# A transformer block with four expert feed-forward rounds: gates to all partitions through a DRAM row, rounds written out

## The chip, the cores and the metric

The kernel runs on one core of one Trainium2 chip. The metric is the device time of one execution, in microseconds. A profile is one execution recorded by the hardware.

## The reference, cut to what matters

Two sequences of 1024 tokens with 128 features go through a block: a layer norm with modulation, attention over pages, a residual, again a layer norm, a feed-forward part, a residual. The change touches the feed-forward part alone:

```python
cur = x                                            # 2048 tokens x 128
for r in range(4):                                 # rounds
    logits = cur @ Wg[r] + bg[r]                   # 4 experts
    vals, idx = top_k(logits, 2)
    w = softmax(vals)
    cw = sum(one_hot(idx, 4) * w[..., None], axis=1)
    hmid = gelu(einsum('nh,ehf->enf', cur, W1) + b1[:, None, :])   # 512 wide
    y = einsum('enf,efh->enh', hmid, W2) + b2[:, None, :]
    cur = cur + einsum('ne,enh->nh', cw, y)
```

All four experts are computed for every token; the gate `cw` weighs them (two are zero). After the last round the result is scaled by a vector `gb` and added to `x`. All is fp32; the expert products are done in three passes of a shorter float type, from a high and a low part of each operand.

## The kernel before, in words

`adaln_block` runs four functions one after the other: `prep`, `attention`, `project` and `ffn`. Only `ffn` is touched (line 869 on).

The 2048 tokens are four chunks of 512 (`CH`), stored with the features on the partitions: `m.cur[:, c, :]`. A chunk takes 16 steps (`K`): four experts by four slices of 128 hidden units. In each step TensorE does `up` (three matmuls of 512 columns into a bank `hid`, lines 939 to 941) and `down` (three matmuls that add into `y`, lines 951 to 953), ScalarE does `gelu` (lines 1010 and 1011: the value, and its high part), VectorE does `low` (line 1042: the low part, from two SBUF inputs). `up` and `gelu` run ahead of `down`: `up(r, s + 3)` stands before `down(r, s)`, and there are four buffers each (`RING`). At the end of an expert VectorE's `combine` (line 1093) adds the bias, multiplies with the gate and writes `part`; GpSimd adds `part` to `cur` (line 1135) and, after the fourth expert, splits `cur` into high and low parts for the next round (lines 1121 and 1123).

The gates of a chunk come in a chain. TensorE's `logits` (line 959) are four fp32 products with only four columns, VectorE's `ranks` (lines 1060 to 1078) are four stages that find the two best experts and the gap between them, ScalarE's `tanh` (line 1021) gives the softmax of two, VectorE's `weights` (lines 1084 and 1086) makes `cw`, with a token on each partition. But `combine` needs a gate for each column, on all 128 partitions. So `spread` (line 969) transposes, for one expert, the gate's column broadcast to 128 by 128, four times for a chunk's 512 tokens, and ScalarE's `keep` (line 1017) copies the bank `pcw` to `cwb`. That is 16 transposes and four copies of 512 columns per chunk.

The order is written by hand as steps relative to a chunk's first step: `LOGITS` at -14, `RANKS` at -13, -11, -10 and -9, `TANH` at -8, `WEIGHTS` at -7, `SPREAD` at -6, -3, 0 and 3, `KEEP` two steps behind each. `due` turns this into steps of the loop. Every engine runs `Fori(0, R)` over the four rounds with 64 steps written out in the body; the waits go by values of the loop's register, and semaphores start with a credit so that the first waits pass. What belongs to the next round is done at the end of a round, also in the last one: there `up` of three steps, `logits`, `ranks` and two spreads belong to a round that does not come. SyncE does nothing here until the end.

After the loop TensorE multiplies each chunk of `cur` with the diagonal of `gb` (line 998), VectorE adds it to `x` (line 1114) and SyncE stores it (line 1145), chunk by chunk.

Of the kernel before, what the change touches and what calls it, by code (L numbers as in the profile page):

```python
# [868 lines left out]
def ffn(nc, m, l):  # L869
# [6 lines left out]
    K = NE * FF // P  # L876
    NS = NCH * K
    AHEAD, RING = 3, 4
    cur_hi = l.sb("cur_hi", [P, NCH, CH], F32R)
# [4 lines left out]
    cwb = l.sb("cwb", [P, NE, CH])  # L884
# [5 lines left out]
    cw = l.sb("cw", [P, TPC, NE])  # L890
# [7 lines left out]
    log_ok, gap_ok, th_ok, cw_ok, pcw_ok, cwb_ok, part_ok, add_ok, chain = (  # L898
        l.sem(n) for n in ("log_ok", "gap_ok", "th_ok", "cw_ok", "pcw_ok", "cwb_ok", "part_ok", "addf_ok", "chain"))
    last_ok, out_ok, stored = (l.sem(n) for n in ("last_ok", "out_ok", "stored"))  # L900

    GEL_CREDIT, Y_CREDIT, PART_CREDIT, ADD_CREDIT, CWB_CREDIT = RING, RING, 2, 2, 1
    LINKS = 10

    def wrap(r, s):
        return (r + 1, s - NS) if s >= NS else (r, s)

    def split_step(s):
        return s // K, s % K // (FF // P), s % (FF // P)

# [7 lines left out]
    def due(steps, s):  # L918

        return [(c, x) for c in range(NCH + 1) for x, at in enumerate(steps) if K * c + at == s]  # L920

    def before(steps):

        return [x for x, at in enumerate(steps) if at < 0]

    with nc.Block() as block:

        @block.tensor
        def _(pe):
            def up(r, s):  # L930

                r, s = wrap(r, s)
                c, e, q = split_step(s)
                if s % K == 0:
                    pe.wait_ge(cur_ok, NCH * r + c + 1)
                pe.wait_ge(gel_ok, NS * r + s - RING + 1 + GEL_CREDIT)
                f = slice(q * P, (q + 1) * P)
                h = hid[s % RING][:, :]
# [4 lines left out]
            def down(r, s):  # L943

                c, e, q = split_step(s)
                n = NE * (NCH * r + c) + e
                if q == 0:
                    pe.wait_ge(part_ok, n - 1 + PART_CREDIT)
                pe.wait_ge(lo_ok, NS * r + s + 1)
                o, x, first, last = y[e % 2][:, :], e * (FF // P) + q, q == 0, q == FF // P - 1  # L950
                nc.tensor.matmul(o, m.w2_hi[:, x, :], gel_hi[s % RING][:, :], start=first, stop=False)  # L951
                nc.tensor.matmul(o, m.w2_lo[:, x, :], gel_hi[s % RING][:, :], start=False, stop=False)  # L952
                nc.tensor.matmul(o, m.w2_hi[:, x, :], gel_lo[s % RING][:, :], start=False, stop=last).then_inc(y_ok, 1)  # L953

            def logits(r, c):
                if not isinstance(r, int):
                    pe.wait_ge(cur_ok, NCH * r + c + 1)
                for i in range(TPC):
                    mm = nc.tensor.matmul(plog[:, i * NE:(i + 1) * NE], m.cur[:, c % NCH, i * P:(i + 1) * P],  # L959
                                          m.wg[:, r + c // NCH, :], start=True, stop=True)  # L960
                mm.then_inc(log_ok, 1)

            def spread(r, c, e):

                n = NE * (NCH * r + c) + e
# [7 lines left out]
            nc.tensor.sem_inc(gel_ok, GEL_CREDIT)  # L973
            nc.tensor.sem_inc(y_ok, Y_CREDIT)
            nc.tensor.sem_inc(part_ok, PART_CREDIT)
            nc.tensor.sem_inc(add_ok, ADD_CREDIT)
            nc.tensor.sem_inc(cwb_ok, CWB_CREDIT)
            logits(0, 0)
            for s in range(AHEAD):
                up(0, s)  # L980
            for e in before(SPREAD):
                spread(0, 0, e)

            with pe.Fori(0, R) as r:
                for s in range(NS):
                    up(r, s + AHEAD)
                    for c, _ in due(LOGITS, s):
                        logits(r, c)
                    for c, e in due(SPREAD, s):
                        spread(r, c, e)  # L990
                    down(r, s)
            for c in range(NCH):

                pe.wait_ge(add_ok, NE * (NCH * (R - 1) + c + 1) + ADD_CREDIT)
                if c == 0:
                    pe.wait_ge(gel_ok, NS * R + 1 + GEL_CREDIT)
                for i in range(TPC):
                    mm = nc.tensor.matmul(hid[(c + 3) % RING][:, i * P:(i + 1) * P], m.cur[:, c, i * P:(i + 1) * P],
                                          m.gbd[:, c // 2, :], start=True, stop=True)
                mm.then_inc(last_ok, 1)  # L1000

        @block.scalar
        def _(act):
            def gelu(r, s):
                r, s = wrap(r, s)
                c, e, q = split_step(s)
                act.wait_ge(hid_ok, NS * r + s + 1)
                act.wait_ge(y_ok, NS * r + s - RING + 1 + Y_CREDIT)
                bias = m.b1[:, e, q:q + 1]
                nc.scalar.activation(gel[s % RING][:, :], hid[s % RING][:, :], ACT.Gelu_apprx_tanh, bias=bias)  # L1010
                nc.scalar.activation(gel_hi[s % RING][:, :], hid[s % RING][:, :], ACT.Gelu_apprx_tanh,  # L1011
                                     bias=bias).then_inc(gel_ok, 1)

            def keep(r, c, e):
                n = NE * (NCH * r + c) + e
                act.wait_ge(pcw_ok, n + 1)
                nc.scalar.activation(cwb[:, e, :], pcw[:, :], ACT.Copy).then_inc(cwb_ok, 1)

            def tanh(r, c):
                act.wait_ge(gap_ok, NCH * r + c + 1)  # L1020
# [4 lines left out]
            gelu(0, 0)  # L1025
            tanh(0, 0)
            for e in before(KEEP):
                keep(0, 0, e)
            with act.Fori(0, R) as r:
                for s in range(NS):  # L1030
                    gelu(r, s + 1)
                    for c, _ in due(TANH, s):
                        tanh(r, c)
                    for c, e in due(KEEP, s):
                        keep(r, c, e)

        @block.vector
        def _(v):
            def low(r, s):
                r, s = wrap(r, s)  # L1040
                v.wait_ge(gel_ok, NS * r + s + 1 + GEL_CREDIT)
                nc.vector.tensor_tensor(gel_lo[s % RING][:, :], gel[s % RING][:, :], gel_hi[s % RING][:, :],  # L1042
                                        ALU.subtract).then_inc(lo_ok, 1)

            def linker(r, c, at):
                at = [at]

                def link(ins):
# [3 lines left out]
                    v.wait_ge(chain, LINKS * (NCH * r + c) + at[0])  # L1052
                return link

            def ranks(r, c, stage):

                link = linker(r, c, [0, 3, 5, 7][stage])
                if stage == 0:
                    v.wait_ge(log_ok, NCH * r + c + 1)
                    link(nc.vector.tensor_tensor(log[:, :, :], plog[:, 0:TPC * NE].rearrange("p (t e) -> p t e", e=NE),  # L1060
                                                 m.bg[:, r + c // NCH, :, :].broadcast_to([P, TPC, NE]), ALU.add))
# [18 lines left out]
            def weights(r, c):  # L1080

                link = linker(r, c, LINKS - 1)
                v.wait_ge(th_ok, NCH * r + c + 1)
                link(nc.vector.tensor_tensor(cw[:, :, :], hdiff[:, :, :], th[:, :, :].broadcast_to([P, TPC, NE]),  # L1084
                                             ALU.mult))
                nc.vector.tensor_tensor(cw[:, :, :], cw[:, :, :], half[:, :, :], ALU.add).then_inc(cw_ok, 1)  # L1086

            def combine(r, c, e):
                n = NE * (NCH * r + c) + e
                v.wait_ge(y_ok, NS * r + K * c + (e + 1) * (FF // P) + Y_CREDIT)  # L1090
                v.wait_ge(cwb_ok, n + 1 + CWB_CREDIT)
                v.wait_ge(add_ok, n - 1 + ADD_CREDIT)
                nc.vector.scalar_tensor_tensor(out=part[:, e % 2, :], in0=y[e % 2][:, :], scalar=m.b2[:, e:e + 1],  # L1093
                                               in1=cwb[:, e, :], op0=ALU.add, op1=ALU.mult).then_inc(part_ok, 1)
# [3 lines left out]
            for stage in range(len(RANKS)):  # L1098
                ranks(0, 0, stage)
# [104 lines left out]
```

## Time and profile before

| | |
|---|---|
| runs | 805.25 us median of 3 (802.18 to 806.52) |
| profiled execution | span 804.3 us from the first to the last instruction; the page gives no other time of it |
| feed-forward part in it | from about 367 us to the end |
| TensorE busy | 720.4 us, 90% of the span |
| VectorE busy | 595.7 us, 74% |
| ScalarE busy | 551.1 us, 69% |
| GpSimd busy | 190.9 us, 24% |
| mean granted TensorE clock | 0.947 of full speed |

PE is TensorE, PEld its weight loads, DVE is VectorE, ACT ScalarE, POOL GpSimd, SPq the queue of SyncE. A matmul's recorded end lies beyond the start of the next one since they overlap; the pace is read from start to start. In a timeline, a row with x4 and one duration merges four instructions of one kind.

### The profile page before, as it was taken

The numbers are of one execution on the slowest core, as the hardware profiler recorded it, in microseconds if no ns is written. First come the engines' busy times: TensorE is split into PE (matmuls) and PEld (weight loads), VectorE is DVE, ScalarE is ACT, GpSimd is POOL, SyncE is SP. The second block draws the span as 40 slices with busy tenths as digits, with TensorE's granted clock in tenths as the row PEclk, the third lists the DMA queues.
The fourth block names the chain that finished last, engine by engine and source line by source line (L and its number), as shares of the span: only waits on it lengthen the run. The fifth ranks groups of instructions, "written<-read, shape, count | busy, mean of one in ns | idle before, by whom it ended". The sixth has DMA issues, their size and how long they took to land.

```text
span 804.3 us, 14061 instructions
## 1 busy us (share of the span) xinstructions
PE 720.4 (90%) x4265; PEld 453.4 (56%) x4265; DVE 595.7 (74%) x1148; ACT 551.1 (69%) x958; POOL 190.9 (24%) x152
## 2 busy tenths in 40 slices
PE   4912897999899999977999999999999999999998
PEld 2400132333333333355777777877787777777786
DVE  5752986888688884095687788777887788777876
ACT  2520054766577768825888888888888888888884
POOL 0541033000000000002233333332333333332333
PEclk9965588999999999996999999999999999999999
DMA  9531040110110100000000000000000000000001
GB/s 239 158 119 50 0 131 22 40 38 12 37 30 15 40 4 2 2 1 0 1 2 1 0 1 0 0 0 0 0 0 0 0 0 0 0 0 0 0 0 52
DMA packets 14580, 20.06 MB, mean 25 GB/s; under 512 B 2794, under 2 KB 10474, under 8 KB 13766
## 3 DMA queue, kind: packets, MB, share of 16 engines
q1 hardware_dynamic: 13221, 17.74, 7.4%
q10 hardware_dynamic: 1312, 1.74, 0.8%
q8 instruction: 26, 0.43, 0.2%
q14 instruction: 21, 0.16, 0.1%
HBM read 15.08 MB, written 4.19 MB: 24 GB/s over the span
## 4 chain that ended last, share of the span: by engine, by line
PE 47%; issue 3%; DVE 2%; ACT 1%; POOL 0%; POOLq 0%; DVEq 0%
PE y L951 8%; PE y L953 7%; PE y L952 7%; PE hid L939 7%; PE hid L941 7%; PE hid L940 7%; PE pcw L969 4%; PE plog L959 2%; ACT gel_hi L1011 1%; DVE cw L1086 0%; DVE cw L1084 0%; DVE gel_lo L1042 0%; POOL cur L1135 0%; POOL cur_lo L1123 0%; DVE hdiff L1076 0%
## 5 line engine op out<-in xcount | busy, mean ns | idle before, releaser
L1042 DVE TENSOR_TENSOR gel_lo<-gel,gel_hi 128x512 fp32r<-128x512 f32 x257 | 254.0, 1027 | 12.7 <-ACT gel_hi L1011 6.7
L588 DVE TENSOR_REDUCE mcol<-mx 128x1 f32<-128x512 f32 (+2 forms) x320 | 193.0, 634 | 62.1 <-PE mx L704 59.1
L562 ACT ACTIVATE probs<-st 128x512 f32<-128x512 f32 x288 | 155.7, 596 | 98.8 <-PE st L660 98.3
L1010 ACT ACTIVATE gel<-hid,b_sb 128x512 f32<-128x512 f32 x257 | 178.1, 693 | 38.6 <-PE hid L941 19.5
L1011 ACT ACTIVATE gel_hi<-hid,b_sb 128x512 fp32r<-128x512 f32 x257 | 176.7, 688 | 0.0
L1135 POOL TENSOR_TENSOR cur<-cur,part 128x512 f32<-128x512 f32 x64 | 105.1, 1643 | 279.7 <-DVE part L1093 279.7
L704 PE MATMUL mx<-ks,qs 125*128 125x512 bf16 (+3 forms) x384 | 120.1, 361 | 40.0 <-PEq L208 32.1
L951 PE MATMUL y<-gel_hi,w_hi 128*128 128x512 f32 x256 | 111.9, 437 | 0.0
L1093 DVE SCALAR_TENSOR_TENSOR part<-y,b_sb,cwb 128x512 f32<-128x512 f32 x64 | 48.1, 751 | 77.3 <-PE y L953 77.3
L939 PE MATMUL hid<-cur_hi,w_hi 128*128 128x512 f32 x259 | 103.7, 400 | 0.0
L941 PE MATMUL hid<-cur_hi,w_lo 128*128 128x512 f32 x259 | 103.5, 400 | 0.0
L940 PE MATMUL hid<-cur_lo,w_hi 128*128 128x512 f32 x259 | 103.5, 400 | 0.0
L704 PEld LDWEIGHTS mx<-ks,qs 125*128 125x128 bf16 x384 | 33.1, 99 | 122.6 <-DVE mcol L588 58.6
L952 PE MATMUL y<-gel_hi,w_lo 128*128 128x512 f32 x256 | 101.5, 396 | 0.0
L953 PE MATMUL y<-gel_lo,w_hi 128*128 128x512 f32 x256 | 101.4, 396 | 0.0
L660 PE MATMUL st<-qs,ks 128*128 128x512 bf16 (+3 forms) x384 | 88.4, 331 | 9.0 <-DMA qs<-mrow 5.3
L681 PE MATMUL ov<-probs,vs 128*32 128x256 f32 (+1 forms) x1280 | 93.2, 373 | 0.4 <-ACT probs L562 0.4
L951 PEld LDWEIGHTS y<-gel_hi,w_hi 128*128 128x128 f32 x256 | 48.5, 189 | 19.1 <-DVE gel_lo L1042 11.4
L941 PEld LDWEIGHTS hid<-cur_hi,w_lo 128*128 128x128 f32 x259 | 49.5, 191 | 11.8
L940 PEld LDWEIGHTS hid<-cur_lo,w_hi 128*128 128x128 f32 x259 | 49.5, 191 | 11.7
L939 PEld LDWEIGHTS hid<-cur_hi,w_hi 128*128 128x128 f32 x259 | 49.2, 190 | 11.8
L953 PEld LDWEIGHTS y<-gel_lo,w_hi 128*128 128x128 f32 x256 | 48.2, 188 | 11.9
(144 smaller groups left out, 620.2 us busy)
## 6 DMA issues: line engine op xcount, KB each, us to landing
ks<-in_k_rows SPq DMA_DIRECT2D x3, 640.0 KB
qs<-in_q_rows SPq DMA_DIRECT2D x3, 616.0 KB
q_pieces<-pieces_q SPq DMA_DIRECT2D x4, 384.0 KB, 4.8
k_pieces<-pieces_k SPq DMA_DIRECT2D x4, 384.0 KB, 6.1
ks<-k_pieces SPq DMA_DIRECT2D x8, 192.0 KB
qs<-q_pieces SPq DMA_DIRECT2D x8, 192.0 KB
x_sb<-in_x SPq DMA_DIRECT2D x4, 256.0 KB, 5.0
ks<-k_pieces SPq DMA_DIRECT2D x8, 128.0 KB
```

Source lines behind the costliest of these rows:

```text
L562: nc.scalar.activation(probs[u % SLOTS][:, h, :], st[:, (HG * u + h) % ST_RING, :], ACT.Exp, scale=SCALE).then_inc(exp_done, 1)
L588: nc.vector.tensor_reduce(mcol[a % SLOTS][:, h, slot:slot + step * (len(blocks) - 1) + 1:step], mx[:, at % MX_RING, 0:len(blocks) * keys]. ...
L704: mm = nc.tensor.matmul(mx[:, at % MX_RING, x * keys:(x + 1) * keys], m.qs[s][0:ROW_MAX, h, t * P:(t + 1) * P], m.ks[s][0:ROW_MAX, h, k0:k ...
L939: nc.tensor.matmul(h, m.w1_hi[:, e, f], cur_hi[:, c, :], start=True, stop=False)
L940: nc.tensor.matmul(h, m.w1_hi[:, e, f], cur_lo[:, c, :], start=False, stop=False)
L941: nc.tensor.matmul(h, m.w1_lo[:, e, f], cur_hi[:, c, :], start=False, stop=True).then_inc(hid_ok, 1)
L951: nc.tensor.matmul(o, m.w2_hi[:, x, :], gel_hi[s % RING][:, :], start=first, stop=False)
L952: nc.tensor.matmul(o, m.w2_lo[:, x, :], gel_hi[s % RING][:, :], start=False, stop=False)
L953: nc.tensor.matmul(o, m.w2_hi[:, x, :], gel_lo[s % RING][:, :], start=False, stop=last).then_inc(y_ok, 1)
L1010: nc.scalar.activation(gel[s % RING][:, :], hid[s % RING][:, :], ACT.Gelu_apprx_tanh, bias=bias)
L1011: nc.scalar.activation(gel_hi[s % RING][:, :], hid[s % RING][:, :], ACT.Gelu_apprx_tanh, bias=bias).then_inc(gel_ok, 1)
L1042: nc.vector.tensor_tensor(gel_lo[s % RING][:, :], gel[s % RING][:, :], gel_hi[s % RING][:, :], ALU.subtract).then_inc(lo_ok, 1)
```

## The change

The four `Fori` loops become straight code over 256 steps `n`, with chunks `k` from 0 to 15; waits are for constants, the credits are gone, and nothing of a fifth round is issued. `spread` and its four copies are replaced: `cw` is laid out by expert first, one transpose (`turn`) makes 16 rows of 128 tokens from it, ScalarE copies them to `cwt`, SyncE writes them to a DRAM row of 8 KB and reads the row back broadcast to all 128 partitions (1 MB) into one of two buffers `cwb`. The steps move: logits at -26, ranks at -25, -23, -22 and -21, tanh at -20, weights at -19, turn at -18, keep at -17. The closing product of a chunk is issued 28 steps after its first step where there are such (three of four), with its residual add and store, and uses the banks `plog` and `pcw`.

```diff
-    cwb = l.sb("cwb", [P, NE, CH])
+    cwb = [l.sb(f"cwb{i}", [P, NE, CH]) for i in range(2)]
-    LOGITS, RANKS, TANH, WEIGHTS = [-14], [-13, -11, -10, -9], [-8], [-7]
-    SPREAD = [-6 + 3 * e for e in range(NE)]
-    KEEP = [-4 + 3 * e for e in range(NE)]
+    LOGITS, RANKS, TANH, WEIGHTS, TURN, KEEP = [-26], [-25, -23, -22, -21], [-20], [-19], [-18], [-17]
+    LAST = [28]
+    EARLY = min(LOGITS)
...
-            def spread(r, c, e):
-                n = NE * (NCH * r + c) + e
-                pe.wait_ge(cw_ok, NCH * r + c + 1)
-                pe.wait_ge(cwb_ok, n + CWB_CREDIT)
+            def turn(k):
+                pe.wait_ge(cw_ok, k + 1)
+                if k >= 1:
+                    pe.wait_ge(cwt_ok, k)
+                nc.tensor.transpose(pcw[0:NE * TPC, 0:P], cw[:, :, :].rearrange("p e t -> p (e t)"),
+                                    m.ident[:, :]).then_inc(turn_ok, 1)
+            def last(c):
+                pe.wait_ge(add_ok, NE * (CHUNKS - NCH + c + 1))
+                if c == 0:
+                    pe.wait_ge(gap_ok, CHUNKS)
+                elif c == 1:
+                    pe.wait_ge(cwt_ok, CHUNKS)
+                else:
+                    pe.wait_ge(out_ok, c - 1)
                 for i in range(TPC):
-                    mm = nc.tensor.transpose(pcw[:, i * P:(i + 1) * P], cw[:, i, e:e + 1].broadcast_to([P, P]),
-                                             m.ident[:, :])
-                mm.then_inc(pcw_ok, 1)
+                    mm = nc.tensor.matmul(last_bank(c)[:, i * P:(i + 1) * P], m.cur[:, c, i * P:(i + 1) * P],
                                           m.gbd[:, c // 2, :], start=True, stop=True)
                 mm.then_inc(last_ok, 1)
+            events(EARLY)
+            for n in range(AHEAD):
+                up(n)
+            for n in range(EARLY + 1, 0):
+                events(n)
+            for n in range(N):
+                if n + AHEAD < N:
+                    up(n + AHEAD)
+                events(n)
+                down(n)
+            last(NCH - 1)
...
-                nc.scalar.activation(cwb[:, e, :], pcw[:, :], ACT.Copy).then_inc(cwb_ok, 1)
+            def keep(k):
+                act.wait_ge(turn_ok, k + 1)
+                if k >= 1:
+                    act.wait_ge(gate_out, 16 * k)
+                nc.scalar.activation(cwt[:, :], pcw[0:NE * TPC, 0:P], ACT.Copy).then_inc(cwt_ok, 1)
...
+            def combine(k, e):
+                n = NE * k + e
+                v.wait_ge(y_ok, Q * (n + 1))
+                if e == 0:
+                    v.wait_ge(gate_in[k % 2], 16 * (k // 2 + 1))
...
+            def spread(k):
+                s = k % 2
+                sp.wait_ge(cwt_ok, k + 1)
+                if k >= 2:
+                    sp.wait_ge(gate_in[s], 16 * (k // 2))
+                sp.dma_start(m.gates[s], cwt[:, :]).then_inc(gate_out, 16)
+                sp.wait_ge(gate_out, 16 * (k + 1))
+                if k >= 2:
+                    sp.wait_ge(part_ok, NE * (k - 1))
+                sp.dma_start(cwb[s][:, :, :].rearrange("p e n -> p (e n)"),
+                             m.gates[s].rearrange("(a r) p -> a (r p)", a=1).broadcast_to([P, NE * CH]))\
+                    .then_inc(gate_in[s], 16)
```

## Rows read from the trace of the kernel before

**Rows 1.** Timeline of TensorE, logits: start us, duration us, engine, line, what.

```profile
384.06 0.95 PE L959 MATMUL plog<-wg_sb,cur 128*128 x8
...
488.30 0.95 PE L959 MATMUL plog<-wg_sb,cur 128*128 x8
...
514.36 0.95 PE L959 MATMUL plog<-wg_sb,cur 128*128 x8
```

**Rows 2.** View of the waits, 384 to 796.8: total us, times, longest.

```profile
DVE part L1093 <- PE y L953: 75.5, 47, 2.2
...
PEld y L951 <- DVE gel_lo L1042: 11.4, 32, 0.4
PE pcw L969 <- DVE cw L1086: 6.4, 16, 0.4
```

**Rows 3.** Timeline of TensorE: a plain step, a spread, logits.

```profile
560.43 0.40 PE L951 MATMUL y<-gel_hi,w_hi 128*128 128x512 f32 x1
...
561.83 0.40 PE L951 MATMUL y<-gel_hi,w_hi 128*128 128x512 f32 x1
...
563.24 0.60 PE L969 MATMUL pcw<-ident,cw 128*128 128x128 f32 x4
563.59 0.48 PE L951 MATMUL y<-gel_hi,w_hi 128*128 128x512 f32 x1
563.91 0.39 PE L952 MATMUL y<-gel_hi,w_lo 128*128 128x512 f32 x1
...
566.47 0.95 PE L959 MATMUL plog<-wg_sb,cur 128*128 x8
567.28 0.48 PE L951 MATMUL y<-gel_hi,w_hi 128*128 128x512 f32 x1
```

**Rows 4.** Timeline, TensorE and VectorE, around the spread of step 10.

```profile
579.16 0.40 PE L941 MATMUL hid<-cur_hi,w_lo 128*128 128x512 f32 x1
...
579.64 0.17 DVE L1086 TENSOR_TENSOR cw<-cw,half 128x16 f32<-128x16 f32 x1
...
579.95 0.65 PE L969 MATMUL pcw<-ident,cw 128*128 128x128 f32 x4 [0.40 <-DVE cw L1086]
```

**Rows 5.** Timeline of VectorE, and of GpSimd (POOL), same chunk.

```profile
563.56 5.09 DVE L1042 TENSOR_TENSOR gel_lo<-gel,gel_hi 128x512 fp32r<-128x512 f32 x4
...
570.36 0.75 DVE L1093 SCALAR_TENSOR_TENSOR part<-y,b_sb,cwb 128x512 f32<-128x512 f32 x1 [1.10 <-PE y L953]
571.02 2.38 DVE L1042 TENSOR_TENSOR gel_lo<-gel,gel_hi 128x512 fp32r<-128x512 f32 x2
573.33 0.21 DVE L1068 TENSOR_TENSOR at_least<-at_least,tri 128x64 f32<-128x64 f32 x1
...
574.06 0.69 DVE L1042 TENSOR_TENSOR gel_lo<-gel,gel_hi 128x512 fp32r<-128x512 f32 x1
...
571.27 1.59 POOL L1135 TENSOR_TENSOR cur<-cur,part 128x512 f32<-128x512 f32 x1 [3.16 <-DVE part L1093]
```

**Rows 6.** Timeline of TensorE and a window (clock after the busy times), the start.

```profile
375.46 0.91 PE L969 MATMUL pcw<-ident,cw 128*128 128x128 f32 x4 [3.12 <-DVE cw L1086]
...
377.89 0.78 PE L939 MATMUL hid<-cur_hi,w_hi 128*128 128x512 f32 x1
...
380.00:382.00 2.00, 2.00 (x7) 1.61 (x6) 1.38 (x2) 2.00 (x5) 0.00 (x0) 0.50 0.00 0
```

**Rows 7.** Timeline, the end: closing products and the last add.

```profile
797.03 3.73 PE L998 MATMUL hid<-gb_diag,cur 128*128 128x128 f32 x32
...
798.21 1.28 POOL L1135 TENSOR_TENSOR cur<-cur,part 128x512 f32<-128x512 f32 x1 [4.38 <-DVE part L1093]
```

**Rows 8.** DMA: issues (KB, us to landing), and instruction packets (packets, MB) from 384 to 796.

```profile
q_pieces<-pieces_q SPq DMA_DIRECT2D x4, 384.0 KB, 4.8
...
w_raw<-in_W SPq DMA_DIRECT2D x1, 1024.0 KB, 5.3
...
q8 instruction: 4, 0.07, 0.1%
```

More of the change, by code:

```diff
@@ L955, in logits, with down @@
-            def logits(r, c):
-                if not isinstance(r, int):
-                    pe.wait_ge(cur_ok, NCH * r + c + 1)
+            def down(n):
+                k, e, q = split_step(n)
+                if q == 0 and NE * k + e >= 2:
+                    pe.wait_ge(part_ok, NE * k + e - 1)
+                pe.wait_ge(lo_ok, n + 1)
+                o, x, first, last = y[e % 2][:, :], e * Q + q, q == 0, q == Q - 1
+                nc.tensor.matmul(o, m.w2_hi[:, x, :], gel_hi[n % RING][:, :], start=first, stop=False)
+                nc.tensor.matmul(o, m.w2_lo[:, x, :], gel_hi[n % RING][:, :], start=False, stop=False)
+                nc.tensor.matmul(o, m.w2_hi[:, x, :], gel_lo[n % RING][:, :], start=False, stop=last).then_inc(y_ok, 1)
@@ L958, in logits @@
+            def logits(k):
+                r, c = divmod(k, NCH)
+                if r >= 1:
+                    pe.wait_ge(add_ok, NE * (k - NCH + 1))
+                if k >= 1:
+                    pe.wait_ge(chain, LINKS * (k - 1) + 1)
                 for i in range(TPC):
-                    mm = nc.tensor.matmul(plog[:, i * NE:(i + 1) * NE], m.cur[:, c % NCH, i * P:(i + 1) * P],
-                                          m.wg[:, r + c // NCH, :], start=True, stop=True)
+                    mm = nc.tensor.matmul(plog[:, i * NE:(i + 1) * NE], m.cur[:, c, i * P:(i + 1) * P],
+                                          m.wg[:, r, :], start=True, stop=True)
@@ L974, in _ @@
[L974 to L998, printed above, removed]
+            def turn(k):
[4 more added lines that the diff above has]
+                                    m.ident[:, :]).then_inc(turn_ok, 1)
@@ L1000, in _, with events @@
                 mm.then_inc(last_ok, 1)
+            def events(n):
+                for k, _ in due(LOGITS, n):
+                    logits(k)
+                for k, _ in due(TURN, n):
+                    turn(k)
+                for k, _ in due(LAST, n, CHUNKS - NCH):
+                    last(k - (CHUNKS - NCH))
+            events(EARLY)
[8 more added lines that the diff above has]
+                down(n)
@@ L1025, in _, with tanh @@
[L1025 to L1035, printed above, removed]
+            def tanh(k):
+                act.wait_ge(gap_ok, k + 1)
+                nc.scalar.activation(th[:, :, :], gap[:, :, :], ACT.Tanh).then_inc(th_ok, 1)
@@ L1037, in _, with low @@
+            gelu(0)
+            for n in range(EARLY, 0):
+                events(n)
+            for n in range(N):
+                if n + 1 < N:
+                    gelu(n + 1)
+                events(n)
         @block.vector
         def _(v):
[L1039 to L1042, printed above, removed]
+            def low(n):
+                v.wait_ge(gel_ok, n + 1)
+                nc.vector.tensor_tensor(gel_lo[n % RING][:, :], gel[n % RING][:, :], gel_hi[n % RING][:, :],
@@ new lines, in result, with events @@
+            def result(c):
+                v.wait_ge(last_ok, c + 1)
+                xs = m.x[:, TPC * c:TPC * (c + 1), :]
+                nc.vector.tensor_tensor(xs, xs, last_bank(c)[:, :].rearrange("p (t e) -> p t e", e=E),
+                                        ALU.add).then_inc(out_ok, 1)
+            def events(n):
+                for k, stage in due(RANKS, n):
+                    ranks(k, stage)
+                for k, _ in due(WEIGHTS, n):
+                    weights(k)
+                for k, _ in due(LAST, n - 1, CHUNKS - NCH):
+                    result(k - (CHUNKS - NCH))
@@ L1096, in _ @@
             v.wait_ge(hi_ok, 1)
             nc.vector.tensor_tensor(cur_lo[:, 0, :], m.cur[:, 0, :], cur_hi[:, 0, :], ALU.subtract).then_inc(cur_ok, 1)
-            for stage in range(len(RANKS)):
-                ranks(0, 0, stage)
-            low(0, 0)
-            weights(0, 0)
-            with v.Fori(0, R) as r:
-                for s in range(NS):
-                    low(r, s + 1)
-                    for c, stage in due(RANKS, s):
-                        ranks(r, c, stage)
-                    for c, _ in due(WEIGHTS, s):
-                        weights(r, c)
-                    if s % (FF // P) == FF // P - 1:
-                        combine(r, *split_step(s)[:2])
@@ L1111, in _ @@
-            for c in range(NCH):
-                v.wait_ge(last_ok, c + 1)
-                xs = m.x[:, TPC * c:TPC * (c + 1), :]
-                nc.vector.tensor_tensor(xs, xs, hid[(c + 3) % RING][:, :].rearrange("p (t e) -> p t e", e=E),
-                                        ALU.add).then_inc(out_ok, 1)
+            for n in range(EARLY, RANKS[0] + K):
+                events(n)
+            low(0)
+            for n in range(RANKS[0] + K, 0):
+                events(n)
+            for n in range(N):
+                if n + 1 < N:
+                    low(n + 1)
+                events(n)
+                if n % Q == Q - 1:
+                    combine(*split_step(n)[:2])
```

149 lines of the change are left out of this document (74 added, 75 removed).

## The prediction

> **What bounds the kernel now.** I read the timeline of TensorE first. In the feed-forward part it issues logits at the same step of every chunk, and these stand 26.06 us apart: (488.30 - 384.06) / 4 and 514.36 - 488.30 agree, although a turn of the loop over the rounds lies in the first stretch and none in the second [rows 1]. So the loop itself costs nothing that can be seen, and the part is 16 equal chunks. The view of the waits says what TensorE lacks inside a chunk: 11.4 us in all before a `down` for `gel_lo`, two such waits per chunk, and 6.4 us for `cw`, one per chunk; VectorE, in turn, waits 75.5 us for `y` [rows 2]. TensorE is the bound, with short hiccups.
>
> Its own timeline prices the pieces. From one `down` to the next there are six matmuls in 1.40 us, 0.2333 each; 96 of them fill 22.4 us of the 26.06 [rows 3]. A `spread` (four transposes) stands between its neighbours for 563.59 - 563.24 = 0.35 us, and the matmul after it starts its successor 0.32 us later where 0.23 is usual, so 0.44 in all. Logits (four fp32 products, eight records) cost 567.28 - 566.47 = 0.81 and the same 0.09: 0.90 [rows 3]. Four spreads are 1.76. Hence 26.06 - 22.40 - 1.76 - 0.90 = 1.0 us of stalls per chunk. The largest is at `spread` of step 10: the last matmul of `up` starts at 579.16, so TensorE is free at 579.39 and the transposes start at 579.95, 0.14 after `cw` is ready (579.64 + 0.17); that is 0.56 [rows 4]. The other 0.4 are the waits for `gel_lo`.
>
> Where these come from stands on VectorE and GpSimd. After a `combine` at 570.36, VectorE does two `low` in 2.38 us, though one alone takes 0.69 (the one at 574.06); GpSimd's add began at 571.27 and ran to 572.86, and the second `low` was done only after it, with the next work of VectorE at 573.33, that is 2.97 us after the start of `combine` [rows 5]. With the two further GpSimd operations at a chunk's end four `low` take 5.09 [rows 5]. So each GpSimd operation with SBUF inputs holds VectorE up by up to its own length.
>
> **The change, part by part.** The sum runs over the stretch from the first logits in the loop (384.06) to the end of the last `down` (the closing products start at 797.03): 412.97 us [rows 1, 7]. By the prices above: 1521 matmuls (254 `down`, 253 `up`) 354.9, 16 logits 14.4, 63 spreads 27.7, 16 x 1.0 stalls 16; 413.0. It closes, so each part can be changed by itself.
>
> 1. *Spreads go.* 63 x 0.44 = -27.7. Two of them, with 13 others, lie ahead of the stretch (below).
> 2. *Turns come.* One transpose for each of the chunks 2 to 15 in the stretch, 14. A transposition among four costs (0.35)/4 = 0.09, and the 0.09 after it: 0.18. 14 x 0.18 = +2.5. Bounds: 0.09 and the whole 0.44 (it now gives 16 rows instead of 128; 128 columns still pass), so 1.3 to 6.2.
> 3. *Work past the end goes.* The old loop wraps: in the last chunk it still issues three `up` of a fifth round (9 x 0.233 = -2.1) and logits, ranks and two spreads of a 17th chunk (the spreads are among the 63). Logits now end with chunk 15, issued in chunk 13: 14 in place of 16, 2 x 0.90 = -1.8.
> 4. *Stalls.* The order of ranks, tanh and weights moves by four steps within a chunk (13 steps plus a chunk), so it keeps its phase to `combine` and to the GpSimd adds: stage 3 again before a `combine`, weights two steps on, and the TensorE instruction that needs `cw` again one step behind it. What queues behind that wait, `down` of step 14, is what stood behind the old `spread` of step 10. So the 0.56 stay, with some 0.3 for `gel_lo` behind the same congestion. The stall of the group of steps 3 to 6 should go: `combine` starts 1.06 us after the `down` it follows, the second `low` is done 2.97 later, and 4.2 us are there (three steps of 1.40), with the logits' 0.90 now before step 6. The group at the chunk's start loses the spreads and logits that had covered it: 1.06 + 0.67 + 5.09 = 6.8 us against five steps, 7.0. It fits, barely. I take 0.85 in the 14 chunks that still carry gates, 0.15 in chunks 14 and 15, which carry none: 12.2, so -3.8. Bounds: no stall at all (-16), and, if each of three lock sites per chunk slips as much as the one of `cw` does, 3 x 0.56 + 0.3 = 2.0 a chunk (+12).
> 5. *Closing products moved into the stream.* Four products in fp32, eight records, 3.73 us for all four chunks at the end [rows 7], so 0.93 and 0.09 each; three of them now stand at step 12 of chunks 13, 14 and 15: +3.1. The first waits for `gap` of chunk 15, one step after VectorE's stage 3, perhaps 0.3, but then takes the `cw` stall of this chunk away: -0.3 net. The residual adds (0.69 us of VectorE each) fall beside it.
> 6. *ScalarE* gives up four copies of 0.60 us per chunk for one of 16 x 128. It wasn't the bound; nothing. *GpSimd* no longer splits the last four chunks' `cur`: nothing on the path.
> 7. *SyncE and the DMA queue* were idle here. Now each chunk writes 8 KB and reads it back as 1 MB. The wait that is new, `combine` of expert 0 on `gate_in`, has every later `low` behind it on VectorE, and so TensorE. No row shows this pair; the nearest are 4.8 us to landing for a 384 KB write to DRAM and 5.3 us for a 1 MB load [rows 8]. With 0.3 for the copy and 1.3 for two issues the way is 12 us. The cover is from `turn` at step 14 of one chunk to `combine` at step 3 of the next but one, 20 steps and the delays in them: about 32 us. Nothing, then; it decides from 32 us on. [...]
>
> Sum over the stretch: -27.7 + 2.5 - 2.1 - 1.8 - 3.8 + 3.1 - 0.3 = -30.1.
>
> *The start.* Before, `cw` of chunk 0 is ready at 375.4, the first two spreads run from 375.46 and `up(3)` starts at 377.89 [rows 6]. Now TensorE does `turn` of chunk 0, then the logits of chunk 1 (about 1.0 us at the lower clock), waits for VectorE's second gate chain (13 small operations and a tanh, some 3.5 us without GpSimd beside them), and turns again; `up(3)` at about 380.6. That is 2.7 later. The spread of step 0 lies before the stretch and in no term above; it goes too, and at the lower clock four transposes had taken about 0.85: 1.9 later. The granted clock stood at 0.50, the 1.2 GHz level, while the work took up again [rows 6]; if it repeats from the later restart, another 0.9 is lost. ScalarE's `gelu(1)` is now behind the copy of chunk 1, but `low(1)` is still in time for `down(1)`. I take +2.5 (2.0 to 4.0).
>
> *The tail.* Of the closing products only chunk 3's remains. It can start when GpSimd's add ends (798.21 + 1.28 = 799.49, plus some 0.1), where it started at 797.03 + 3 x 0.93 = 799.82 [rows 7]: -0.2, the last store following as before. Bounds -0.5 to +0.9 (the same product at the lower clock after 2.6 us of idling).
>
> All: -30.1 + 2.5 - 0.2 = -27.8 against the profiled execution, whose span is 804.3; the page gives no other time of it. That makes 776.5. The median of the runs lies 0.95 above that span, so the time is 805.25 - 27.8 = 777.4.
>
> **Rivals.**
>
> *A. VectorE's congestion takes a part back.* A chunk costs VectorE, its waits for GpSimd included, about 5.09 + 3 x (2.38 + 2 x 0.69) for the `low`, 3.0 for four `combine` and 2.9 for the gates, 22 us in all [rows 5]; TensorE now asks for it in 24.3 rather than 26.06, with less slack in each group of four steps. For it: the group at the chunk's start fits by 0.2 us only. Against: VectorE still waits 75.5 us for TensorE today. Price: one more half-length lock (0.64) in 14 chunks, 9 us: 786.4.
>
> *B. Nearly no stalls.* If, with the spreads gone the stalls don't recur (the ring of four and three steps ahead absorb them): 14 x 0.85 = 12 less, 765.5. Against: the phase to `combine` is kept.
>
> *C. Straight-line code starves the sequencers (the slower side).* Four times the code passes once. Between 384 and 796 the trace shows 4 packets of instructions on one of two such queues [rows 8] and no stall that repeats per round. With the other queue alike, three times 8 fresh ones come, 24, and now 1 MB loads stand beside them in the same DMA engines; if each held TensorE for one such load, 5.3 us, that is 127 us, and already 6 of them (32 us) cancel the gain. At 9 of 24: 777.4 + 48 = 825. Against: prefetch has a whole chunk's time for each. In "Runtime: NRT & Kernel Launch" (Trainium skill, section "Instruction fetch mechanics") prefetch is sequential and a taken branch beyond the window costs a stall, so straight code should win a little; the trace shows no such cost at the loop turn [rows 1], so I give it nothing.
>
> *D. The gates come late.* Should the way through DRAM take over 32 us, every chunk waits. From 36 us on the gain is gone (two stalls share one excess); at 40: about 4 us x 14 = 56, 833. For: nothing in rows 8. Against: three times the rows' sum is needed. It would not "do what it says", since the DMA would set the pace.
>
> **How the numbers follow.** Forecast (770 to 782) 0.60; A 0.22; B 0.10; C 0.04; D 0.02; a stall of a kind not thought of that leaves no gain 0.02. A time of 777 is the likeliest. The range to hold 8 in 10 takes in A, B and most of the way to the stall bounds: 766 to 794. With what this kernel's runs spread (802.18 to 806.52), 0.5% is 4 us: faster 0.93, within 0.5% 0.02, slower 0.05.
>
> **What would show it.** Logits 24.3 to 24.4 us apart in chunks 1 to 13 and about 22.6 to 23.6 for the last two chunks; one transpose per chunk at about 0.2; a wait for `cw` of some 0.5 in each of 14 chunks; no wait of `combine` for a DMA; the write and read of the gates landing within 12 us; `up(3)` some 2.7 us later after the first gates; three stores some 20, 40 and 60 us before the end. I am wrong if `combine` waits on `gate_in`, if TensorE's waits show "issue" in new places, if `gel_lo` waits exceed 1.5 us a chunk, or if the first `down` comes later than 385.

## The result and the profile after

The changed kernel takes 770.65 us, median of four runs (769.32 to 774.71), against 805.0. The ratio is 0.958, with an interval of 0.955 to 0.962: 4.2% faster. Forecast were 777.4, in 766 to 794. The direction and the range held; the gain was 34 us where 28 were forecast, and the reason for the difference is the instructive part.

From the page of the kernel after: the span, and the busy times of its engines.

```profile
span 770.1 us, 12222 instructions
...
PE 681.2 (88%) x3976; PEld 427.2 (55%) x4000; DVE 588.5 (76%) x1133; ACT 520.4 (68%) x905; POOL 183.8 (24%) x144
```

TensorE is still the bound. Its timeline, logits (L963) and closing products (L984), answers to [rows 1, 7]:

```profile
391.65 0.95 PE L963 MATMUL plog<-wg_sb,cur 128*128 128x4 f32 x8
...
415.56 0.95 PE L963 MATMUL plog<-wg_sb,cur 128*128 128x4 f32 x8
...
534.96 0.95 PE L963 MATMUL plog<-wg_sb,cur 128*128 128x4 f32 x8
...
558.85 0.95 PE L963 MATMUL plog<-wg_sb,cur 128*128 128x4 f32 x8
...
735.00 1.05 PE L984 MATMUL pcw<-gb_diag,cur 128*128 128x128 f32 x8
...
758.37 1.05 PE L984 MATMUL plog<-gb_diag,cur 128*128 128x128 f32 x8
...
762.73 0.39 PE L954 MATMUL y<-gel_lo,w_hi 128*128 128x512 f32 x1
...
763.99 1.26 POOL L1157 TENSOR_TENSOR cur<-cur,part 128x512 f32<-128x512 f32 x1 [3.63 <-DVE part L1105]
...
765.31 1.33 PE L984 MATMUL pcw<-gb_diag,cur 128*128 128x128 f32 x8 [2.18 <-POOL cur L1157]
```

From logits to logits a chunk takes 558.85 - 534.96 = 23.9 us, not 26.06 and not the 24.3 to 24.4 of the forecast; the last, without gates, takes 758.37 - 735.00 = 23.4, closing product included. The view of the waits from 384 us on answers to [rows 2]:

```profile
DVE part L1105 <- PE y L954: 53.3, 38, 1.6
...
PEld pcw L972 <- DVE cw L1096: 9.1, 13, 0.7
...
PE pcw L972 <- DVE cw L1096: 3.4, 13, 0.3
...
PEld y L952 <- DVE gel_lo L1049: 1.2, 2, 0.7
```

The 32 waits for `gel_lo` (11.4 us) have become two, both at the very end; the wait for `cw` is left in 13 chunks. It is seen in the timeline of one chunk, VectorE first, then TensorE, against [rows 4, 5]:

```profile
565.08 0.21 DVE L1075 TENSOR_TENSOR at_least<-at_least,tri 128x64 f32<-128x64 f32 x1
...
565.72 0.69 DVE L1049 TENSOR_TENSOR gel_lo<-gel,gel_hi 128x512 fp32r<-128x512 f32 x1
...
571.13 0.19 DVE L1096 TENSOR_TENSOR cw<-cw,half 128x16 f32<-128x16 f32 x1
...
570.73 0.39 PE L943 MATMUL hid<-cur_hi,w_lo 128*128 128x512 f32 x1
...
571.38 0.28 PE L972 MATMUL pcw<-ident,cw 128*16 128x128 f32 x1 [0.26 <-DVE cw L1096]
571.41 0.48 PE L952 MATMUL y<-gel_hi,w_hi 128*128 128x512 f32 x1
```

TensorE is free at 570.73 + 0.23 = 570.96 and goes on at 571.38: 0.42 lost. The turn itself holds it for 571.41 - 571.38 = 0.03, and 0.09 more on the next matmul. So a chunk is 96 x 0.2333 + 0.90 + 0.12 + 0.42 = 23.84, and 0.04 stay open. And VectorE's second stage of ranks, from its start to the next `low`, takes 565.72 - 565.08 = 0.64, where it took 574.06 - 573.33 = 0.73 before [rows 5].

The start, against [rows 6], TensorE and the queue of SyncE in the timeline:

```profile
376.50 0.28 PE L972 MATMUL pcw<-ident,cw 128*16 128x128 f32 x1 [3.35 <-DVE cw L1096]
...
377.11 0.33 SPq L1170 DMA_DIRECT2D gate_rows<-cwt  x1
...
378.47 0.35 SPq L1174 DMA_DIRECT2D cwb<-gate_rows  x1
...
381.21 0.38 PE L972 MATMUL pcw<-ident,cw 128*16 128x128 f32 x1 [3.28 <-DVE cw L1096]
...
381.25 0.77 PE L941 MATMUL hid<-cur_hi,w_hi 128*128 128x512 f32 x1
```

The feed-forward part began 1.3 us later in this execution (its first cast at 368.12, before 366.84), so `up(3)` is 2.1 us later in its own time. The two transfers of a chunk, from the DMA view of 384 to 757 us (KB, us to landing), against [rows 8]:

```profile
cwb<-gate_rows SPq DMA_DIRECT2D x14, 1024.0 KB, 4.7
...
gate_rows<-cwt SPq DMA_DIRECT2D x14, 8.0 KB, 1.3
```

### The profile page after: what moved, and what is told of

Read it like the earlier page. It is cut to its first block, busy times and chain, and to the rows that moved or that the text cites. A ratio compares the mean times of both kernels' runs of the same rounds, so it can differ in the third digit from the quotient of the medians.

```text
span 770.1 us, 12222 instructions
## 1 busy us (share of the span) xinstructions
PE 681.2 (88%) x3976; PEld 427.2 (55%) x4000; DVE 588.5 (76%) x1133; ACT 520.4 (68%) x905; POOL 183.8 (24%) x144
## 4 chain that ended last, share of the span: by engine, by line
PE 33%; DVE 12%; issue 5%; ACT 1%; POOL 0%; POOLq 0%; DVEq 0%
DVE gel_lo L1049 6%; PE y L952 6%; PE y L954 5%; PE y L953 5%; PE hid L943 5%; PE hid L942 5%; PE hid L941 5%; PE plog L963 2%; DVE part L1105 1%; ACT gel_hi L1017 1%; DVE at_least L1077 1%; PE pcw L972 1%; DVE cw L1096 0%; DVE cw L1094 0%; DVE dl L1084 0%
## 5 line engine op out<-in xcount | busy, mean ns | idle before, releaser
L1049 DVE TENSOR_TENSOR gel_lo<-gel,gel_hi 128x512 fp32r<-128x512 f32 x256 | 248.3, 1010 | 6.7 <-ACT gel_hi L1017 5.7
L1016 ACT ACTIVATE gel<-hid,b_sb 128x512 f32<-128x512 f32 x256 | 176.1, 688 | 38.5 <-PE hid L943 16.2
L1017 ACT ACTIVATE gel_hi<-hid,b_sb 128x512 fp32r<-128x512 f32 x256 | 174.7, 682 | 0.0
L952 PE MATMUL y<-gel_hi,w_hi 128*128 128x512 f32 x256 | 104.4, 408 | 0.4 <-DVE gel_lo L1049 0.2
L660 PE MATMUL st<-qs,ks 128*128 128x512 bf16 (+3 forms) x360 | 82.8, 327 | 13.8 <-DMA qs<-mrow 6.6
L1105 DVE SCALAR_TENSOR_TENSOR part<-y,b_sb,cwb 128x512 f32<-128x512 f32 x64 | 47.8, 747 | 53.3 <-PE y L954 53.3
L660 PEld LDWEIGHTS st<-qs,ks 128*128 128x128 bf16 x384 | 34.4, 99 | 37.6 <-issue 14.8
```

What stands on the lines that cost most here:

```text
L952: nc.tensor.matmul(o, m.w2_hi[:, x, :], gel_hi[n % RING][:, :], start=first, stop=False)
L1016: nc.scalar.activation(gel[n % RING][:, :], hid[n % RING][:, :], ACT.Gelu_apprx_tanh, bias=bias)
L1017: nc.scalar.activation(gel_hi[n % RING][:, :], hid[n % RING][:, :], ACT.Gelu_apprx_tanh, bias=bias).then_inc(gel_ok, 1)
L1049: nc.vector.tensor_tensor(gel_lo[n % RING][:, :], gel[n % RING][:, :], gel_hi[n % RING][:, :], ALU.subtract).then_inc(lo_ok, 1)
```

## The experiments

The ratio of each is to the kernel before, measured beside it on the same chip; the changed kernel's is 0.958. Where a kernel was run once, its ratio is left out and the distance of its logits decides, which within a trace, e8 apart, repeats to 0.03 us from chunk to chunk.

### e1: the rounds written out, nothing else

```diff
-            with pe.Fori(0, R) as r:
+            for r in range(R):
...
-            with act.Fori(0, R) as r:
+            for r in range(R):
...
-            with v.Fori(0, R) as r:
+            for r in range(R):
...
-            with pool.Fori(0, R) as r:
+            for r in range(R):
```

> The kernel before with its four loops written out, all waits constant, nothing else: 66 spreads, the fifth round's work and the old steps stay. By the forecast the loop costs nothing: 805 (803 to 807), logits 26.06 apart, 1.0 us of stalls a chunk. By the rival (a wait for a register's value puts an instruction ahead of it, and VectorE's small gate operations pay for it): the gaps ahead of the low after stages 1, 2 and 3 shrink by about 0.08 each, VectorE comes to the combine of step 7 some 0.3 earlier, and of the stalls 0.4 to 0.5 a chunk go: logits 25.6 apart, about 798.

It took 799.45, ratio 0.990 (0.986 to 0.993). Timeline and waits:

```profile
538.29 0.95 PE L959 MATMUL plog<-wg_sb,cur 128*128 128x4 f32 x8
...
563.85 0.95 PE L959 MATMUL plog<-wg_sb,cur 128*128 128x4 f32 x8
```

```profile
PEld y L951 <- DVE gel_lo L1042: 0.8, 3, 0.5
```

25.56 us a chunk: 0.49 less than before, in 16 chunks 7.8 us. All but three waits for `gel_lo` are gone with no transpose removed, and of the 1.0 us of stalls a chunk 25.56 - 22.40 - 1.76 - 0.90 = 0.5 are left. The rival holds as to the gain; the forecast's "the loop itself costs nothing that can be seen" was read from the turn of the loop only, and that does cost nothing.

### e6 and e7: which engine's loop

e6 writes out VectorE's loop alone (the third edit of e1), e7 TensorE's alone (the first).

> The kernel before with VectorE's loop alone written out; the other engines keep their loops and register waits. If what the rounds written out gave (0.49 us a chunk, 26.06 to 25.57) comes from VectorE's waits between its small gate operations, nearly all of it is here: logits 25.6 apart, about 7 us faster than the kernel before. If it comes from TensorE's own register work, or from all engines alike: 26.0, within 2 us.

> The kernel before with TensorE's loop alone written out. By the theory that VectorE's waits are the cause: logits 26.0 to 26.06 apart, no gain. By the rival that TensorE's register instructions ahead of its waits delay it after a stall (0.1 for each of three stalls): 25.7.

e6 took 797.46, ratio 0.990 (0.987 to 0.993). Its timeline, two logits, and VectorE from its second stage to the `low` behind it:

```profile
533.53 0.95 PE L959 MATMUL plog<-wg_sb,cur 128*128 x8
...
559.17 0.95 PE L959 MATMUL plog<-wg_sb,cur 128*128 x8
...
540.20 0.21 DVE L1068 TENSOR_TENSOR at_least<-at_least,tri 128x64 f32<-128x64 f32 x1
...
540.58 0.22 DVE L1070 TENSOR_TENSOR at_least<-at_least,above 128x64 f32<-128x64 f32 x1
540.84 0.69 DVE L1042 TENSOR_TENSOR gel_lo<-gel,gel_hi 128x512 fp32r<-128x512 f32 x1
```

The last operation of the same stage in the kernel before, ahead of the `low` at 574.06 [rows 5]:

```profile
573.72 0.22 DVE L1070 TENSOR_TENSOR at_least<-at_least,above 128x64 f32<-128x64 f32 x1
```

e7 took 805.13 in its one run; two logits:

```profile
514.16 0.95 PE L959 MATMUL plog<-wg_sb,cur 128*128 128x4 f32 x8
...
540.14 0.95 PE L959 MATMUL plog<-wg_sb,cur 128*128 128x4 f32 x8
```

VectorE alone gives 26.06 - 25.64 = 0.42 a chunk, TensorE alone 0.08; together 0.50, which is e1's 0.49. So the cause is VectorE's loop, but for 0.08 that no run follows further. In e6 the stage takes 0.64 again, and in e7, where VectorE keeps its loop, 0.73.

Where the time goes can be read from start to start, alike in all 16 chunks. Inside a stage nothing changes, although each operation waits for the one before it: 573.72 - 573.47 = 0.25 in the loop, 540.58 - 540.33 = 0.25 without. The difference is ahead of the `low` behind the stage, 574.06 - 573.72 = 0.34 against 540.84 - 540.58 = 0.26, where two waits follow each other, for the stage's last result and for `gel`. Behind `weights`, where one wait stands, `low` follows after 0.10 in both. The trace also records the register instructions, which the timeline leaves out: in the loop one of 0.04 us, at the line of `low`'s own wait, carries the wait for the stage's result; it starts at 573.98, and `low` 0.08 behind it. In e6 `low` carries this wait itself, and the one for `gel` is a plain wait that starts at 540.59, ahead of it. Inside the stage the register instruction starts at 573.73, beside the operation of 573.72, and costs nothing. So it is the register work for the second of two waits that shows, since it comes after the first wait has ended.

It adds up over a chunk. Stages 1 to 3 take 0.73, 0.62 and 0.58 up to what follows them, in e6 0.64, 0.53 and 0.52. A `combine` has three waits: behind stage 3 it starts 1.05 us after the start of the last matmul it needs, in e6 0.76, and the other three of a chunk come 0.15 to 0.20 sooner too. With them go GpSimd's add and the `low` that is held up until this add ends.

### e5: the transfers left out

```diff
-            for k in range(CHUNKS):
+            for k in range(2):
                 spread(k)
```

The waits for the transfers that are gone are changed to match. The kernel leaves out 14 of the 16 transfers and with them the right gates of 14 chunks: these take the gates of the first two.

> The changed kernel with the DRAM way for the first two chunks only; the other 14 chunks use these two sets of gates again, so 14 writes and 14 broadcasts of 1 MB are left out (turns and copies stay). If the transfers cost the engines nothing: logits 23.88 apart, as in the changed kernel, 770 within 2. If 1 MB into SBUF beside the work slows it: nearer, up to 0.5 us a chunk.

```profile
533.07 0.95 PE L963 MATMUL plog<-wg_sb,cur 128*128 128x4 f32 x8
...
556.95 0.95 PE L963 MATMUL plog<-wg_sb,cur 128*128 128x4 f32 x8
```

23.88 us a chunk, and 770.21 for the one run: 14 broadcasts of 1 MB beside the work cost nothing that can be measured.

### e9: the transposes put back

They read the unit matrix in place of the gates, and nobody reads their output.

```diff
+            def extra(n):
+                if n < (CHUNKS - 2) * K and n % K in (0, 3, 10, 13):
+                    pe.wait_ge(cwt_ok, n // K + 2)
+                    for i in range(TPC):
+                        nc.tensor.transpose(pcw[:, i * P:(i + 1) * P], m.ident[:, :], m.ident[:, :])
...
+                if n >= 0:
+                    extra(n)
```

> The changed kernel with 16 transposes of 128 by 128 put back into each of the first 14 chunks, at the steps of the old spreads (0, 3, 10, 13), with no copy and no reader: their output is left out of the result. If a spread is worth 0.44 on TensorE whatever stands beside it: 4 x 0.44 = 1.75, logits 25.6 apart, 770 + 25 = 795. If those at steps 10 and 13 partly fill the wait for cw at step 14 (0.42): 25.2 to 25.3 apart, 790.

```profile
546.03 0.95 PE L963 MATMUL plog<-wg_sb,cur 128*128 128x4 f32 x8
...
571.25 0.95 PE L963 MATMUL plog<-wg_sb,cur 128*128 128x4 f32 x8
```

25.22 a chunk, 792.92 for the one run, and no wait for `cw` on TensorE is left in its view of the waits. So 16 transposes are worth 1.34, not 1.76: the 0.42 that TensorE lost ahead of `turn` are filled by them. The price per spread fits; about a quarter of what removing them freed (0.42 of 1.76) turned into waiting for VectorE.

### e3 and e8: how far ahead the gates must be

e3 sets the steps back to those of before; its other edits keep the banks of the closing products apart.

```diff
-    LOGITS, RANKS, TANH, WEIGHTS, TURN, KEEP = [-26], [-25, -23, -22, -21], [-20], [-19], [-18], [-17]
+    LOGITS, RANKS, TANH, WEIGHTS, TURN, KEEP = [-14], [-13, -11, -10, -9], [-8], [-7], [-6], [-5]
```

e8 is e3 with:

```diff
                 sp.dma_start(m.gates[s], cwt[:, :]).then_inc(gate_out, 16)
-                sp.wait_ge(gate_out, 16 * (k + 1))
+                for j in range(8):
+                    sp.wait_ge(gate_out, 16 * (k * 9 + j + 1))
+                    sp.dma_start(m.gates[s], cwt[:, :]).then_inc(gate_out, 16)
+                sp.wait_ge(gate_out, 16 * (k + 1) * 9)
```

> The changed kernel with its gate chain 12 steps later (logits 14 steps ahead, as in the kernel before), same phase to combine. From the write of the row to the landing of the broadcast it took 7.4 us, from turn about 8; eight steps are left, 11 to 12 us. If the 26 steps ahead are needed to cover the DRAM way, combine of expert 0 waits for gate_in in each chunk, by up to some us, and it is slower by 10 us or more. If the way fits: no wait, the chunks stay 23.9 apart, and the second gate chain leaves the start: up(3) comes 4.4 us earlier, less what the first combine then waits for its gates (landing at 383.5, needed at 384): 4 us faster than the changed kernel, about 767.

> e3 (gates 14 steps ahead) with each chunk's row written nine times, one after the other, ahead of the broadcast: 8 more of 1.35 us each, 10.8 us on a way that was 6.8 from turn to landing, where 14.5 are there. If late gates are paid in full by combine of expert 0 and by all that stands behind it on VectorE: an excess of about 3 us in each of 15 chunks, logits 26.9 apart, 768 + 45 = 813, slower than the kernel before. If the rings of four and three steps ahead absorb a part: less than half of that.

e3 took 768.31, ratio 0.950 (0.947 to 0.954):

```profile
523.99 0.95 PE L965 MATMUL plog<-wg_sb,cur 128*128 128x4 f32 x8
...
547.89 0.95 PE L965 MATMUL plog<-wg_sb,cur 128*128 128x4 f32 x8
```

23.90 a chunk and no wait for a transfer: 14 steps ahead are enough. From the feed-forward part's first operation, ScalarE's cast of `cur`, to the last `down` it needs 759.25 - 366.68 = 392.6 us, the changed kernel 762.73 - 368.12 = 394.6: 2.0 less, where 4 were expected. `up(3)` does come 4.7 us sooner after the cast. Of the 2.7 that are lost again, 1.4 are the second chunk's logits, turn and wait for `cw` (0.90 + 0.12 + 0.42), which leave the start only to stand in the stream. Some 0.7 are the clock: from `up(3)` to `down` of step 2, logits left out, e3 takes 5.5 us and the changed kernel 4.8, with the granted clock at 0.50 for the first 4 us in e3 and for the first 2.6 in the changed kernel. The rest is open. The intervals of the two ratios, up to 0.954 and from 0.955, just don't overlap, which agrees.

e8 took 846.51 in its one run. View of its waits, a `combine` in its timeline, and two matmuls of TensorE 1.8 us and more after the same wait:

```profile
DVE part L1109 <- DMA cwb<-gate_rows: 66.1, 15, 10.0
```

```profile
505.64 0.75 DVE L1109 SCALAR_TENSOR_TENSOR part<-y,b_sb,cwb 128x512 f32<-128x512 f32 x1 [4.79 <-DMA cwb<-gate_rows]
```

```profile
508.84 0.69 PE L953 MATMUL y<-gel_hi,w_hi 128*128 128x512 f32 x1
509.33 0.63 PE L954 MATMUL y<-gel_hi,w_lo 128*128 128x512 f32 x1
```

Late gates are paid in full, 66.1 / 15 = 4.4 us a chunk, and more: its span is 77 us longer than that of e3, 5.2 for each of 15 chunks, where 3 were expected. Two things were put too low. The way without the extra writes is 7.7 us and not 6.8 (in e3 a turn at 560.44, the broadcast issued at 563.44, 4.7 to landing); the eight writes themselves delay the broadcast by 10.0 us, a little less than the 10.8 expected. And the clock was left out: after TensorE has stood still for the gates, its matmuls are 0.43 to 0.49 apart for a while instead of 0.23. The mean granted clock from 384 to 836 us is 0.94, where e3 has 1.00 from 384 to 759. Some 95 such matmuls, counted in its timeline, make about 18 of the 77 us. The mechanism of rival D is real; nothing of it was in the changed kernel.

### e4: the turn a step later

```diff
-    LOGITS, RANKS, TANH, WEIGHTS, TURN, KEEP = [-26], [-25, -23, -22, -21], [-20], [-19], [-18], [-17]
+    LOGITS, RANKS, TANH, WEIGHTS, TURN, KEEP = [-26], [-25, -23, -22, -21], [-20], [-19], [-17], [-16]
```

> The changed kernel with turn and its copy one step later, two behind weights. In the changed kernel TensorE waits 0.42 us a chunk ahead of turn. If it waits for cw alone, the wait shrinks to what gel_lo of the same step asks (ready 0.1 after TensorE is free): 0.3 x 14 = 4 us faster, 766 to 767. If gel_lo of that step is as late as cw (both are behind the same GpSimd add), the wait only changes its name: within 1 us.

It took 769.48, ratio 0.952 (0.948 to 0.956), which the whole time can't tell from the changed kernel; 766 to 767 were expected.

```profile
535.53 0.95 PE L963 MATMUL plog<-wg_sb,cur 128*128 128x4 f32 x8
...
559.17 0.95 PE L963 MATMUL plog<-wg_sb,cur 128*128 128x4 f32 x8
```

```profile
PEld y L952 <- DVE gel_lo L1049: 6.2, 15, 0.7
```

23.65 us a chunk: 0.23 gained, and the rest of the 0.42 is now a wait for `gel_lo` of the same step. TensorE is free at 571.28, the `low` ends at 571.33, and with the slower start of the matmul behind the wait 0.2 us are lost. Neither theory alone: `cw` came last, but `gel_lo` came late as well; this `low` took 1.53 us instead of 0.69, with GpSimd's add beside it until 570.78.

### e2: closing products at the end

```diff
-    LAST = [28]
+    LAST = []
...
     def last_bank(c):
-        return pcw if c % 2 else plog
+        return hid[(c + 3) % RING]
...
-            last(NCH - 1)
+            for c in range(NCH):
+                last(c)
```

> The changed kernel with all four closing products, their adds and stores after the last step, in the four hidden banks as before. If the early stores are a gain, this is slower than the changed kernel by up to 3 us (three stores of 0.9 us each at the end). If they are a loss: three products of 0.93 + 0.09 us leave the busy stretch and fill TensorE's wait of some 2.5 us for the last add, and the waits of the last steps for gel_lo behind a residual add (1.2 us) go too: -3 to -4 in the stretch, 0 to +1 at the end, so 2 to 4 us faster than the changed kernel, about 768.

It took 771.0, ratio 0.954 (0.950 to 0.958). The whole time can't tell it from the changed kernel, and 768 was expected. From the last logits to the last `down` it needs 763.85 - 705.21 = 58.6 us, the changed kernel 762.73 - 702.12 = 60.6: 2.0 less. From there to the end of the span 7.55 against 7.37: 0.2 more. TensorE's wait for `low` in the last steps, in its view of the waits:

```profile
PEld y L952 <- DVE gel_lo L1046: 1.6, 2, 1.2
```

So early stores are a small loss, 1.8 us by one profile each: three products then run inside TensorE's wait for the last add, where they are free. Their price is 3 x 0.89 = 2.7; the 0.7 that don't show are waits for the last `gel_lo`, the longest 1.2 instead of 0.7, which the product at step 252 had covered.

### b1: the three together

> The changed kernel with three edits together: gates 14 steps ahead (e3), turn and copy one step later (e4), all four closing products after the last step (e2). If their gains add: e3 gave 2.0 us from the first cast to the last down, e4 0.23 us a chunk (now 15 chunks, 3.4), e2 2.0 in the stretch less 0.2 at the end: 7 us in all, 770.7 - 7 = 763.5, logits 23.66 apart. If they meet the same slack (VectorE behind GpSimd's adds), the chunks stay at 23.9 and it is 767.

It took 762.57 (761.33 to 765.08), ratio 0.947 (0.943 to 0.950), with

```profile
523.70 0.95 PE L963 MATMUL plog<-wg_sb,cur 128*128 128x4 f32 x8
...
547.36 0.95 PE L963 MATMUL plog<-wg_sb,cur 128*128 128x4 f32 x8
```

23.66 a chunk, and 754.59 - 368.13 = 386.5 us from the first cast to the last `down`, 8.1 less than the changed kernel. The gains add, as expected (763.5), and its interval lies below that of the changed kernel.

## Why the prediction was right, and where its size was off

The stretch that the sum was made over, from before `down` of step 2 (386.03) to the end of the last `down` (762.96), takes 376.9 us: -36.0 against 412.97, forecast -30.1. By the same prices its work is 1512 matmuls (352.8), 14 logits (12.6), 14 turns (1.7) and three closing products (2.7); 7.2 are left for stalls.

1. *Spreads*, -27.7: the price of 0.44 fits. e9 finds 1.34 for four instead of 1.76, and the difference is the wait for `cw`, 0.42, which stands here only without them; the forecast has it as a stall, in term 4. The prediction's "two of them, with 13 others, lie ahead of the stretch" is a slip: 66 are issued, three of them before the stretch, and the 63 are those inside it.
2. *Turns*, +2.5: 0.12 each, 14 make 1.7. The forecast's 0.18 was 0.8 too much in all.
3. *Work past the end*, -3.9: gone as said. The logits are 14 and no `up` of a fifth round is there.
4. *Stalls*, -3.8: this is the term that was mis-sized. Put at 12.2, they are 7.2: 0.46 in each of 13 chunks and 1.2 in the last two. That is -8.8 against the 16 of before, and 5.0 of the missing 5.9 us; the turns are 0.8 and the closing products 0.1. The step that failed is "it keeps its phase to `combine` and to the GpSimd adds ... So the 0.56 stay, with some 0.3 for `gel_lo`", and under it "the loop itself costs nothing that can be seen". The phase in steps is kept (it moved by 12 steps, not by the "13 steps plus a chunk" of the prediction), but not VectorE's speed through it: written out, its gate stages are 0.24 us shorter and its `combine` start 0.15 to 0.3 sooner (e6), the waits for `gel_lo` are gone and the one for `cw` is 0.42. e1 has the same 0.5 of stalls a chunk with all spreads in place, so the writing out alone brings them down to this. That the group of steps 3 to 6 would cease to stall, and that five steps at a chunk's start just fit, came out; but e1 loses these stalls too with the steps where they were, so the reasons that the forecast gave for it aren't shown.
5. *Closing products*, +2.8: 0.80 + 0.09 each, 2.7. That VectorE's residual adds "fall beside it" was not quite right: the `low` of the last step stands behind one (760.83, 0.68 us), and TensorE waits for this `low` until 762.16. It is in term 4 above.
6. *ScalarE, GpSimd*: nothing, as said.
7. *DMA*: nothing, as said (e5). The way was put at 12 us. At the start it is 378.47 + 4.7 - 377.11 = 6 us from the first write's issue; in the stream 7.9 us from the turn (571.38, write at 571.98, broadcast at 574.63, 4.7 to landing). There the broadcast is issued after a `combine` has ended (573.80 + 0.75) that frees its buffer. The cover was more than twice what it needed to be (e3). The read's 4.7 us lie below the 5.3 of the row.

*Start*: forecast +2.5, measured (386.03 - 368.12) - (384.06 - 366.84) = +0.7. The second gate chain went as said, 381.21 - 376.50 = 4.7 between the turns; but the granted clock was back at 1.00 from 384 us on, 2.6 us behind the start of `up(3)`, where it had taken some 4.6 before. The 0.9 kept for it fell away. e2 and e4, which run the same code here, had 0.50 until 386, and their first logits in the stream came 24.4 to 24.5 us after the first cast instead of 23.5: executions differ here by one us, so that the small loss of this one is in part luck. *Tail*: -0.2 forecast, 770.1 - 762.96 = 7.14 against 7.27, -0.1. The rest of the two spans' difference, +1.3, lies ahead of the feed-forward part, which the change doesn't touch: -36.0 + 0.7 - 0.1 + 1.3 = -34.1, and the spans, 804.3 and 770.1, differ by 34.2.

Of the rivals, B ("nearly no stalls", 765.5) was half true, for a reason it didn't name. A is refuted for this kernel: the chunks are shorter than forecast and not longer, and with four spreads less VectorE still waits 53.3 us for `y`. C is refuted: straight code shows no new wait, and e1 is faster by it. D is refuted for this cover: no `combine` waits for a transfer. Of the Trainium skill's "Runtime: NRT & Kernel Launch", section "Instruction fetch mechanics", the prediction took that a taken branch out of the fetched window stalls, and so that straight code should win a little. The sign was right, but no run here shows such a stall: the chunks with a turn of the loop in them are as long as the others, and the gain is VectorE's register work between two waits (e6).

## What to carry to other kernels

Price removed work by what its neighbours do with the gap: of 1.76 us of transposes 0.42 turned into a wait for the next engine in line. Where an engine does small operations in a loop and two or more waits for semaphores follow each other, compare the gap there with that of straight code before calling the loop free; the turn of the loop says nothing on it. And a wait at the end for a last result is a good place for other closing work: moved early, into a stream that TensorE bounds, three products cost 2.0 of their 2.7 us (e2).

## What the runs showed of the hardware that I had not expected

- A wait for a register's value costs VectorE about 0.09 us more than one for a constant where it is the second of two waits behind a small operation (0.34 against 0.26 up to `low`, before and e6), and nothing where it is the only one (0.25 inside a stage, 0.10 behind `weights`, in both).
- Ahead of a `combine`, with three waits, the same costs 0.15 to 0.2 us (0.59 and 0.69 after the last matmul's start against 0.44 and 0.49).
- A transpose of 128 x 16 to 16 x 128 holds TensorE for 0.03 us beside its neighbours, 0.12 with the slower matmul behind it, though its own duration reads 0.28.
- 1 MB broadcast from an 8 KB DRAM row lands in 4.7 us, where a plain load of 1 MB took 5.3, and slows no engine that it could be seen (e5).
- After a wait of TensorE from 502.9 to 507.0 its matmuls were 0.43 us apart for some 3 us instead of 0.23 (e8, mean granted clock 0.94 where e3 has 1.00): a late transfer cost more than its wait.
